# Second attention of a two-layer cross-attention kernel: eight slots of weighted sums in three batches, more of the exponentials' sums on VectorE, and the ending's additions spread

## What is computed

```
x = L0(x, ctx)       # 8 heads of 16: softmax(QK/4)V, W_o, residual, two-layer relu network, residual
# L1, 16 heads of 32:
q  = layernorm(x) @ Wq.T ;  k, v = split(layernorm(ctx) @ Wkv.T)
attn = softmax(q k^T * 32**-0.5)                    # for each head: 4096 x 3202
out  = (attn @ v) per head, joined to 512 features
x = x + out @ Wo.T + bo
h = silu(x @ W1.T + b1)                             # 2048 hidden features
x = x + h @ W2.T + b2
```

## Time and profile before

| what | value |
|---|---|
| median of 3 runs (lowest to highest) | 5515.28 us (5510.59 to 5517.87) |
| profiled execution, its own time | 5516.99 us |
| span of its trace | 5515.2 us |
| TensorE busy, share of the span | 5316.3 us, 96% |
| VectorE busy | 4010.2 us, 73% |
| ScalarE busy | 3172.4 us, 58% |
| GpSimd busy | 2345.2 us, 43% |
| mean granted TensorE clock | 0.977 of 2.4 GHz |

### The profile page before, as it was taken

How to read it: one execution, slowest core, us unless ns; L and a number is a source line. 1 busy time by engine, 2 the same in 40 slices (tenths; PEclk the granted TensorE clock), 3 DMA queues, 4 the chain that set the end, 5 groups by cost and what they waited for, 6 DMA issues and landing times. The chain is left out here.

```text
span 5515.2 us, 93900 instructions
## 1 busy us (share of the span) xinstructions
PE 5316.3 (96%) x28684; PEld 3344.6 (61%) x28684; DVE 4010.2 (73%) x6936; ACT 3172.4 (58%) x5792; POOL 2345.2 (43%) x1165
## 2 busy tenths in 40 slices
PE   8999999999799899999999999999999996999999
PEld 6744444444477565666666666656666663777777
DVE  6689999999477788888888888888888886332331
ACT  4268888888433466666666666666666663322222
POOL 0000000000000488888888888888888885000000
PEclk9989999999799899999999999999999998999999
DMA  7521111111333311111111111111111112322220
GB/s 216 130 48 38 38 38 38 38 38 31 111 120 115 101 40 30 41 39 42 41 28 41 41 42 40 28 42 41 39 42 28 41 28 62 120 87 69 92 84 23
DMA packets 329592, 324.44 MB, mean 59 GB/s; under 512 B 185744, under 2 KB 193808, under 8 KB 327184
## 3 DMA queue, kind: packets, MB, share of 16 engines
q1 hardware_dynamic: 329232, 319.92, 21.9%
HBM read 219.18 MB, written 100.53 MB: 58 GB/s over the span
## 5 line engine op out<-in xcount | busy, mean ns | idle before, releaser
L444 DVE TENSOR_REDUCE a_maxes<-a_mscore 128x1 f32<-128x458 f32 (+4 forms) x5376 | 3038.1, 624 | 590.5 <-PE a_mscore L502 559.1
L427 ACT ACTIVATE a_prob<-a_score 128x512 f32<-128x512 f32 x4992 | 2635.3, 598 | 1175.1 <-PE a_score L511 1162.1
L511 PE MATMUL a_score<-a_q,a_k 97*128 97x512 f32 (+1 forms) x4992 | 1980.2, 432 | 10.9 <-ACT a_prob L427 7.7
L502 PE MATMUL a_mscore<-a_k,a_qm 96*128 96x458 f32 (+4 forms) x5376 | 1893.1, 415 | 36.0 <-DMA a_k<-k 34.4
L530 PE MATMUL a_acc<-a_prob,a_v 128*32 128x512 f32 x9984 | 1601.0, 604 | 0.0
L502 PEld LDWEIGHTS a_mscore<-a_k,a_qm 96*128 96x128 f32 (+1 forms) x5376 | 1475.7, 310 | 159.9 <-DVE a_maxes L444 48.6
L393 POOL TENSOR_TENSOR a_added<-a_added,a_prob 128x1024 f32<-128x1024 f32 x640 | 1534.4, 2397 | 71.0
L511 PEld LDWEIGHTS a_score<-a_q,a_k 97*128 97x128 f32 (+1 forms) x4992 | 917.9, 193 | 970.7 <-ACT a_prob L427 525.5
L525 PE MATMUL a_acc<-a_prob,a_ones 128*1 128x512 f32 x2048 | 961.0, 591 | 0.0
L292 POOL MEMSET a_k<- 32x126 f32 (+4 forms) x6 | 6.3, 1053 | 1819.8 <-POOLq L60 1819.5
L530 PEld LDWEIGHTS a_acc<-a_prob,a_v 128*32 128x32 f32 x9984 | 292.5, 109 | 299.9 <-issue 154.7
(11 more groups left out here) (205 smaller groups left out, 3983.4 us busy)
## 6 DMA issues: line engine op xcount, KB each, us to landing
a_qm<-q SPq DMA_DIRECT2D x384, 64.0 KB, 1.9
a_q<-q SPq DMA_DIRECT2D x384, 64.0 KB, 1.9
acc<-a_acc_sb SPq DMA_DIRECT2D x384, 64.0 KB
e_part<-acc SPq DMA_DIRECT2D x90, 256.0 KB, 3.4
a_k<-k SPq DMA_DIRECT2D x48, 416.0 KB, 6.2
q<-m_qout SPq DMA_DIRECT2D x128, 128.0 KB, 2.3
e_wo<-wo_split SPq DMA_DIRECT2D x32, 512.0 KB, 4.3
k<-kv_k1out SPq DMA_DIRECT2D x24, 512.0 KB, 2.9
```

Source lines behind the costliest of these rows:

```text
L427: act.activation(prob[:, t], score[SCORES[it.j][t]][:], ACT.Exp, scale=SCALE).then_inc(exp_done, 1)
L444: dve.tensor_reduce(maxes[j][:, t, c:c + 1], mscore[u % UNIT_BANKS][:, 0:wide], AX.X, ALU.max).then_inc(unit_read, 1)
L502: pe.matmul(mscore[u % UNIT_BANKS][:, 0:wide], qm[j][r:r + ROW, t:NB:NB // P], kt[kk][r:r + ROW, at:at + wide], start=True, stop=True).the ...
L511: pe.matmul(score[SCORES[it.j][t]][:], kt[it.k][r:r + C, i * P:(i + 1) * P], qt[it.j][r:r + C, :], start=True, stop=True).then_inc(score_d ...
```

## The change

In a1 group 3 carries values in the first two slots, so that eight slots hold all 26 tiles; the fourth group's values are copied out on their own (`copy_side`) behind batch 0, stored as a fourth part, and then the group is used for the ones. Ones cover only tiles 8, 9, 23, 24 and 25 (25 as a full matmul against a column with two ones). VectorE adds six tiles (2 to 4 and 5 to 7) within the same item, in pieces of 256 queries, and GpSimd the rest. The batches are three, and the lists of units and places are new. In `ending` there are four parts to add instead of three, the additions stand at other steps, and the first load of each block is issued earlier. In both attentions the splitting of weights in the last item starts at tile 0 instead of tile 4.

```diff
-            self.ROWS, self.SIDE, self.SUMS = 128, 3, 1
-            self.slots = [[(0, 3 * i), (1, 3 * i + 1), (2, 3 * i + 2), (3, ("one", 3 * i))] for i in range(8)]
-            self.slots.append([(0, 24), (1, 25), (3, ("sum", None))])
-            self.batches = [[0, 1], [2, 3], [4, 5], [6, 7], [8]]
-            self.at = {3: (3, True), 9: (4, True), 14: (0, False), 19: (1, False), 25: (2, False)}
-            self.copy_at = 5
+            self.ROWS, self.SIDE, self.SUMS = 128, 4, 1
+
+            self.slots = [[(c, 4 * i + c) for c in range(4)] for i in range(2)]
+            for i in range(2, 8):
+                first = 8 + 3 * (i - 2)
+                what = [("one", 8), ("one", 9), ("one", 23), ("one", 24), ("rest", 25), ("sum", None)][i - 2]
+                self.slots.append([(0, first), (1, first + 1), (2, first + 2), (3, what)])
+            self.batches = [[0, 1], [2, 3, 4], [5, 6, 7]]
+            self.at = {8: (1, True), 14: (2, True), 18: (0, False)}
+            self.copy_at, self.side_at = 16, 19
+
+            self.sum_at = (8, 11, 12, 17)
...
-            more = dict(enumerate([2, 1, 1, 0, 1, 2, 1, 1, 1, 0, 1, 2, 1, 1, 1, 1, 1, 2, 1, 1, 1, 1, 2, 1, 1, 0]))
+            more = dict(enumerate([2, 0, 2, 1, 0, 1, 1, 1, 1, 1, 2, 1, 1, 1, 1, 1, 0, 2, 2, 1, 1, 1, 1, 2, 0, 1]))
...
-ADDS = 9
-ON_VECTOR, PIECES = range(22, 25), 4
-READ_BY = 7
+
+ADDS, READ_BY, SUMS_READ = 9, (1, 4, 7), 8
+ON_VECTOR, PIECES = (range(2, 5), range(5, 8)), 2
+VSUMS = len(ON_VECTOR) * PIECES
...
+                if APART:
+                    sp.wait_ge(side_copied, n + 1)
+                    sp.dma_start(acc_out[ATEND, bass.ds(h * hd, hd), cols], side[3 * 32:P, :]).then_inc(side_stored, 16)
...
-                for i in range(1, 7):
-                    pool.wait_ge(exp_done, it.n * ST + 3 * i + 3)
-                    if i == 1:
+                for i, t in enumerate((10, 12, 14, 16, 18, 20)):
+                    pool.wait_ge(exp_done, it.n * ST + t + 2)
+                    if i == 0:
                         if not it.first:
                             pool.wait_ge(add_done, base)
-                        pool.tensor_tensor(added[:], prob[:, 1:3], prob[:, 4:6], ALU.add).then_inc(add_done, 1)
+                        pool.tensor_tensor(added[:], prob[:, 0:2], prob[:, 10:12], ALU.add).then_inc(add_done, 1)
...
+                pool.wait_ge(exp_done, it.n * ST + 23)
                 pool.wait_ge(add_done, base + 6)
-                pool.tensor_tensor(added[0:LAST_KEYS, 1], added[0:LAST_KEYS, 1], prob[0:LAST_KEYS, 25],
-                                   ALU.add).then_inc(add_done, 1)
+                pool.tensor_tensor(added[:, 0], added[:, 0], prob[:, 22], ALU.add).then_inc(add_done, 1)
+                pool.wait_ge(vsum_done, it.n * VSUMS + VSUMS)
                 pool.wait_ge(add_done, base + 7)
+                pool.tensor_tensor(added[:], added[:], vsum[:], ALU.add).then_inc(add_done, 1)
+                pool.wait_ge(add_done, base + 8)
...
+            def copy_side(n):
+
+                act.wait_ge(pv_done, n * NBATCH + 1)
+                act.wait_ge(side_stored, n * 16)
+                act.activation(side[3 * 32:P, :], acc[3 * 32:P, :], ACT.Copy).then_inc(side_copied, 1)
...
-            def add_up(n, i):
-
+            def add_up(n, first, which, i):
+
+                tiles = ON_VECTOR[which]
                 if i == 0:
-                    dve.wait_ge(exp_done, n * ST + ON_VECTOR[-1] + 1)
-                    dve.wait_ge(add_done, n * ADDS)
+                    dve.wait_ge(exp_done, n * ST + tiles[-1] + 1)
+                    if which == 0 and not first:
+
+                        dve.wait_ge(add_done, n * ADDS - ADDS + SUMS_READ)
...
-    SUM_AT, HALF_AT, A_AT, ADD_AT = (1, 3, 5, 7), (2, 4, 6, 8), (10, 11, 12, 13), (11, 12, 13, 14)
+
+    SUM_AT = [(1, 3, 5, 7)] + [(0, 3, 6, 9)] * (BLOCKS - 1)
+    HALF_AT = [(2, 4, 6, 8)] + [(1, 4, 7, 10)] * (BLOCKS - 1)
+    A_AT, ADD_AT = (11, 12, 13, 14), (12, 13, 14, 15)
...
-                    for k in range(KT) if n > 0 else ():
+                    for k in range(1, KT) if n > 0 else ():
                         next_acc(n + 1, k)
                     for d in range(KT):
                         load_wo(n + 1, d)
+                if n + 2 < BLOCKS:
+
+                    next_acc(n + 2, 0)
```

More of the change, by code:

```diff
@@ L126, in __init__ @@
         self.opens = {min(ts): b for b, ts in enumerate(tiles)}
-        self.closes = [max(ts) for ts in tiles]
+        summed = [[t[1] for i in b for _, t in self.slots[i] if isinstance(t, tuple) and t[0] != "sum"]
+                  for b in self.batches]
+        self.closes = [max(ts + ones) for ts, ones in zip(tiles, summed)]
         self.units_at, made = [], 0
@@ L403, in _ @@
                 pool.tensor_tensor(total[:], added[:, 0], added[:, 1], ALU.add).then_inc(add_done, 1)
-                pool.wait_ge(add_done, base + 8)
-                pool.wait_ge(vsum_done, it.n * PIECES + PIECES)
-                pool.tensor_tensor(total[:], total[:], vsum[:], ALU.add).then_inc(add_done, 1)
         @block.scalar
@@ L484, in _ @@
                             maximum(it.n + 2, it.j, it.use + 1, u)
-                    if APART and t < PIECES and not it.first:
-                        add_up(it.n - 1, t)
-                if APART and it.last:
-                    for i in range(PIECES):
-                        add_up(it.n, i)
+                    if APART and t in L.sum_at:
+                        add_up(it.n, it.first, *divmod(L.sum_at.index(t), PIECES))
             if weights:
@@ L517, in weigh @@
                     pe.wait_ge(acc_copied, n)
+                if b == 1 and APART:
+                    pe.wait_ge(side_copied, n + 1)
                 pe.wait_ge(exp_done, n * ST + L.closes[b] + 1)
@@ L520, in weigh @@
                     for c, what in L.slots[i]:
-                        after = [x for later in L.slots[i + 1:] for x, _ in later if x == c]
+                        kind = lambda x: isinstance(x, tuple)
+                        same = [j for j, slot in enumerate(L.slots) for x, w in slot if x == c and kind(w) == kind(what)]
+                        start, stop = i == same[0], i == same[-1]
                         if isinstance(what, tuple):
+                            col = 1 if what[0] == "rest" else 0
                             if what[0] == "sum":
                                 pe.wait_ge(add_done, n * ADDS + ADDS)
-                            mm = pe.matmul(acc[c * 32:c * 32 + 1, :], ones[:],
+                            mm = pe.matmul(acc[c * 32:c * 32 + 1, :], ones[:, col:col + 1],
                                            total[:] if what[0] == "sum" else prob[:, what[1]],
-                                           start=(i == 0), stop=not after)
+                                           start=start, stop=stop)
                             continue
@@ L530, in weigh @@
                         mm = pe.matmul(acc[c * 32:c * 32 + 32, :], vt[kk][:, L.FIRST[half] + at, :],
-                                       prob[:, what], start=(i == 0), stop=not after)
+                                       prob[:, what], start=start, stop=stop)
                 mm.then_inc(pv_done, 1)
@@ L1218, in ending @@
         h = [sb(f"h{i}", [P, NB], F32) for i in range(2)]
+        total = h[1]
+        assert H * T // P == NB
         hh = [sb(f"hh{i}", [P, NB], F32R) for i in range(2)]
@@ L1244, in part_of, with recip_part @@
             return part, 0, 2 + (n - 1) * KT + k
+        def recip_part(n, k):
+            return h[0][:] if n == 0 and k % 2 else part[:, SIDE]
         @block.sync
```

67 lines of the change are left out of this document (35 added, 32 removed).

## The result

| | before | after |
|---|---|---|
| median (lowest to highest, executions) | 5512.93 us (5502.76 to 5517.87, 4) | 5614.38 us (5603.3 to 5624.6, 4) |
| profiled execution, span of its trace | 5515.2 us | 5622.8 us |

The ratio is 1.0186, with a 95% interval of 1.0161 to 1.0211: the change makes the kernel 1.9% slower, where 2% less was predicted, and the time lies outside the range.

A forecast was written before the change was run, and what follows sets the result against it. TensorE bounds the kernel before; afterwards two loops and GpSimd's floor (20.65, 20.7, 20.45 us) give 20.8 us an item. -109 + 4 + 4 - 9.5 = -110 from 5517 gives 5407, as median 5405 us; 8-in-10 range 5345 to 5470.

The forecast's parts named there:

- SyncE's queue: In a1 the row's transfer behind the item's stores: landed by 13.4 us, needed at 13.9, so hidden with 0.5 to spare.
- E: First score behind the batch at tile 18, counted from that behind tile 8's batch: 9.75 us without a stall.
- Rival 4: In a1, row or loads late by 0.7 us an item eat the gain: no change 0.04, slower 0.03 more.
- TensorE's part: In a1, eight slots in three batches take 7.9 us instead of 9.4; TensorE alone would need 20.1 us an item.
- VectorE's sums: In a1, a sum of 768 elements takes 0.91 us, with 1.02 kept; an item 18.9 to 19.4 us of VectorE.
- Rival 2: In a1, VectorE's sums of 768 cost 1.1 to 1.4 us, giving 5435 to 5515 us; chance 0.15.
- GpSimd: In a1, seven large additions and two small, 20.45 us an item, are a floor for the period.
- Rival 3: In a1, VectorE's sums slow GpSimd's additions, its work reaching 21.95 us an item: 5554 us; chance 0.05.
- The loop over ScalarE: In a1, 16 scores in a row at ScalarE's pace, from tile 18's batch to tile 8's: a period of 20.7 us.
- The end of a1: Earlier splitting of weights slows GpSimd: 39 us from item 127's first score to the last total, 35 before: +4 us.
- The ending's start: Between a1 and the ending, one more addition in each of four `normalise` and issue of parts: +4 us, not hidden.
- Its blocks: In the ending's blocks, load waits of 12.4 us go and later splits of X add 3: net -9.5 us.

The follow-up runs named there:

- experiment 1: The changed kernel with two alternating side buffers, each with its own semaphore, instead of one: 5531.01 us, ratio 1.0032 to the kernel before.
- experiment 2: The changed kernel, still one side buffer, with the side's store issued ahead of the three other stores: 5513.17 us, ratio 1.0001 to the kernel before.
- 3, side last: The changed kernel, one side buffer, with the side's store issued behind the store of the sums: 5677.09 us, ratio 1.0305 to the kernel before.
- experiment 4: The changed kernel with two side buffers and, in a1, all of move_row ahead of the item's stores: 5460.51 us, ratio 0.9908 to the kernel before.
- experiment 5: The changed kernel with two side buffers, the row's store ahead of the five stores and its load behind them: 5465.12 us, ratio 0.9914.
- experiment 6: The changed kernel, one side buffer; SyncE issues side's store, row's store, three stores, sums' store, row's load last: 5475.18 us, ratio 0.9939.

## Why the prediction was wrong

**The step that failed is "SyncE's queue".** It costed only what comes last in that queue, the row, and found 0.5 us to spare. The side's copy was costed as 0.6 us of ScalarE's work. That it must wait until the side of the item before has been stored, by a store that starts four places down the queue and behind ScalarE's own copy at tile 16, was never worked out. The prediction's own numbers give it: the accumulator's copy done at about 7.7, 1.27 us for three stores, and from its issue 1.6 us until the side's store has landed (the 1.6 that the prediction took for the row's load): 10.6. The side's copy was put at E, 9.75 without a stall. So it is late by 0.8 us in each item (0.4 if E is 10.2, as the 13.9 of the row has it); the traces show 0.7, as 3.36 us behind the accumulator's copy instead of 2.67 (experiment 1). Moving that store up took 101 us off (experiment 2), taking the wait away 83 (1), and moving it down by 0.42 us put 63 on (3).

**The same step was wrong on the row.** The row's load was issued where it was forecast: 4.1 us behind the accumulator's copy in experiment 1, by the prediction 9.8 + 1.97 - 7.7 = 4.1 (but with the row's store at 2.5 instead of 2.1, and 1.43 from there instead of 1.97). What was mis-sized is the load itself: 1.6 us was taken for it, which no row shows, and it took 2.47 in the median there, and 2.29 in the kernel before. So the row was there at 6.5 instead of 5.7, and it was needed at 6.1 (forecast 6.2). 0.9 us more for the load, where 0.5 were to spare, made the row late in 77 items. Taking it out of the way gives 70 us (1 against 4). Rival 4 named this, "the row or the loads are late by 0.7 us an item", with 0.04 for no change and 0.03 for slower: the right queue, the wrong transfer first, and far too small a chance.

**What a wait costs was undercounted.** The prediction let a late transfer cost what it is late, item by item. The periods of the first 125 items of a1 in the profiled executions, with the clock that the trace records for each ("low" are items in which it was at 0.50 for a part):

| | before | changed | 1, two buffers | 2, side first | 3, side last | 4, row too |
|---|---|---|---|---|---|---|
| items over 23.5 us | 0 | 26 | 8 | 7 | 33 | 0 |
| low items | 0 | 28 | 12 | 9 | 33 | 0 |
| us at 0.50 | 0 | 205 | 58 | 38 | 242 | 0 |
| mean of the others, us | 21.66 | 21.73 | 21.42 | 21.45 | 22.03 | 21.20 |

Every late item is a low one. Between the changed kernel and experiment 4 lie 154 us by the medians of the executions, and 172 in these 125 items of the profiled ones, of which the changed kernel's was the slowest of its four. 0.53 us in every item (21.73 for 21.20) make 66 of the 172; the other 106 lie in the 28 low items. My estimate of the clock's share of these 106 is some 65 us: the pair of items above gives 2.2 us for 6.8 us at 0.50, and there are 205 us of it. The rest is the gaps. Rival 4's and the main case's way of counting has no term for the clock.

**TensorE's part:** right. A batch of three takes 2.70 us by the trace, as 3 x 0.86 + 0.13.

**VectorE's sums:** 0.95 us, between the 0.91 taken and the 1.02 kept. Rival 2 (1.1 and more) is out. **GpSimd:** floor right (2.45 and 2.53 us an addition). Rival 3, additions stretched by sums, is out: 2392 ns each, with all four sums beside them. The Trainium skill ("SBUF — State Buffer", the part on the shared port pair) states that on trn2 tensor_reduce never contends with GpSimd, and the trace agrees.

**The loop over ScalarE:** right in kind, 0.4 us short. The timeline of TensorE in experiment 5, one item, first scores and batches:

```profile
3017.85 0.50 PE L542 MATMUL a_score<-a_q,a_k 97*128 97x512 f32 x1
...
3021.19 0.63 PE L568 MATMUL a_acc<-a_prob,a_v 128*32 128x512 f32 x3
...
3027.98 0.50 PE L542 MATMUL a_score<-a_q,a_k 97*128 97x512 f32 x1
...
3031.92 0.47 PE L542 MATMUL a_score<-a_q,a_k 97*128 97x512 f32 x1 [0.36 <-ACT a_prob L448]
...
3036.35 0.63 PE L568 MATMUL a_acc<-a_prob,a_v 128*32 128x512 f32 x3
...
3039.06 0.50 PE L542 MATMUL a_score<-a_q,a_k 97*128 97x512 f32 x1
```

E is 3027.98 - 3017.85 = 10.13 us (9.65 + x forecast, and x, GpSimd's lateness, was 0.1 here); from E to tile 0 it is 3.94 (3.7), from there to the batch 4.43 (4.1), the batch 2.71. The sum is 21.21, where 20.7 was worked out and 20.8 taken. The stretch to the first batch alone is 3.34 for 3.0. Each term is short by what scores and units lose to each other where I had them run at ScalarE's or TensorE's own pace. With both waits mended a1 gives 0.47 us an item, not 0.86: 60 us instead of 109.

**The end of a1:** +4 forecast. The last two items took 49.6 us before, 6.3 more than two median ones, and 48.3 in experiment 5, 5.9 more. So about nothing. GpSimd's additional work was counted; that the splitting of weights now starts 10 us earlier against the end (46 us before the last copy, 36 before), so that it slows item 126's additions more and the last item's less (14.24 us for five, before 17.70), was not.

**The ending's start:** +4 forecast. TensorE stands 45.5 us between a1 and the ending, before 40.0: +5.5, right in kind. **Its blocks:** -9.5 forecast. The splits of X are 101.17 us apart in the later blocks, 102.3 in the mean before, so -1.2 for each; the first block takes 2 us more (103.18 for 101.21). From the last copy of a1 to the end it is 873.1 us, and 873.0 before: zero, where start and blocks together were forecast at -5.5.

## What to carry to other kernels

When a change puts a copy into a buffer that is stored by DMA, work out that buffer's round trip (issue behind what stands in the queue, landing, the next copy) as a loop of its own beside the engines'; here it set the period, and an issue 0.42 us later in it cost 63 us of the program. Take each duration from the median and the maximum of many transfers and not from one: 1.97 us was one item's, and the median 1.43. Order a queue of DMAs by when each is waited for, not by which data belong together: experiment 6 changes nothing but the order and turns 1.9% slower into 0.6% faster. And a wait of an engine in front of another's batch may be where its idle time belongs: look at what the work behind it would collide with before moving it.

## What the runs showed of the hardware that was not expected

- The same store of 64 KB from 32 partitions, 128 times in the changed kernel, is listed in the tile view of `a_side` with these lines, the first of which has the issue on SyncE's queue in ns and the second the way to landing:

```profile
L350 SPq DMA_DIRECT2D acc<-a_side x128: 314/420/1855, 1881.7 to 4751.7; - x128
DMA to landing us min/median/max: 1.6/1.7/4.0
```

  Both tails matter. Of the 26 late items ahead of the last two, 17 have one issue of a store that took 1.2 to 2.1 us, and in eight others the side's store landed 2.8 to 4.0 us behind its issue. A plan made with the medians leaves them out. What made these issues and landings slow stays open. In experiment 4 seven issues took over 1 us too, and with slack in the buffers none of the first 125 items is late.
- The granted clock was at 0.50 through the 9 us behind a gap of 2.05 us in TensorE's work, where it had worked without a break from 3003.39 to 3017.60 ahead of it; behind a gap of 1.71 us it was at 0.50 for 6.8 us, and behind one of 1.77 it stayed at 1.00. In a1 as a whole it was 0.96 with 28 such items and 1.00 before.
- The load of the row, 2 KB that a store has just written, took 2.4 us to land (median) where it was issued the moment that store had landed (experiment 4), and 1.4 where it was issued 1.5 us later, with other stores in between (experiment 5).
